# A decoder layer on one core: the second attention pass with two heads' keys on the partitions

## What is computed

```python
x = layernorm(x + block(x))        # rmsnorm, mamba (scan over 1024 steps, 16 states, 1024 inner channels), rmsnorm, SwiGLU
x = layernorm(x + cross(x, ctx))   # attention to 64 context tokens, below
x = layernorm(x + x @ W.T + b + lora)   # dense layer and a top-2 mixture of 8 rank-16 adapters

# cross attention, 16 heads of 32 channels, 64 keys
qk = einsum('bhqd,bhkd->bhqk', Q, K)
scores = qk / sqrt(32)
feats = [scores.mean((q, k)), scores.max(k).mean(q), var(softmax(scores), k).mean(q)]   # per batch and head
t = exp(clip(mlp(feats), -log 10, log 10))
attn = softmax(qk / (2 * t))
out = einsum('bhqk,bhkd->bhqd', attn, V) -> linear Wo, bo
```

## Time and profile before

| | |
|---|---|
| median of 3 runs | 4376.36 us (4375.86 to 4382.17) |
| profiled execution | 4379.0 us, span 4377.2 us |
| PE busy | 3725.6 us, 85% of the span, 9848 matmul records |
| VectorE busy | 2522.7 us, 58% |
| ScalarE busy | 2161.6 us, 49% |
| GpSimd busy | 2488.3 us, 57% |
| granted TensorE clock, mean | 0.901 of full speed |

### The profile page before, as it was taken

How to read it: one execution, slowest core, us unless ns; L and a number is a source line. 1 busy time by engine, 2 the same in 40 slices (tenths; PEclk the granted TensorE clock), 3 DMA queues, 4 the chain that set the end, 5 groups by cost and what they waited for, 6 DMA issues and landing times.

```text
span 4377.2 us, 36093 instructions
## 1 busy us (share of the span) xinstructions
PE 3725.6 (85%) x9848; PEld 1749.1 (40%) x9848; DVE 2522.7 (58%) x3319; ACT 2161.6 (49%) x5177; POOL 2488.3 (57%) x1100
## 2 busy tenths in 40 slices
PE   6555999799979988899999998899998988899677
PEld 3111434343334334544344334534444333544344
DVE  2665478657756883367735885267744886122211
ACT  3443454565465454556526555466526554443344
POOL 0998399649954993079914994059932996000000
PEclk9555999899989998899999998899999998899788
DMA  4333344334523541144423442134423442112000
GB/s 147 115 113 101 104 155 156 111 120 154 164 95 113 164 157 59 63 140 144 152 86 111 155 153 77 63 121 147 146 84 103 160 154 89 40 57 67 25 21 28
DMA packets 221267, 483.17 MB, mean 110 GB/s; under 512 B 31884, under 2 KB 32268, under 8 KB 220812
## 3 DMA queue, kind: packets, MB, share of 16 engines
q1 hardware_dynamic: 221068, 480.87, 34.3%
HBM read 470.82 MB, written 9.96 MB: 110 GB/s over the span
## 4 chain that ended last, share of the span: by engine, by line
PE 54%; POOL 16%; DVE 12%; issue 8%; ACT 8%; DMA 1%; SPq 0%; POOLq 0%; DVEq 0%; ACTq 0%
PE ps L1490 28%; POOL hb L961 10%; DVE hb L1296 6%; POOL hb L951 6%; PE ps L1579 5%; PE ps L1548 5%; PE ps L1591 5%; PE ps L1658 1%; PE ps L1624 1%; PE ps L1603 1%; PE ps L1541 1%; PE ps L1518 1%; ACT ps L1171 1%; PE ps L1670 1%; PE ps L1559 1%
## 5 line engine op out<-in xcount | busy, mean ns | idle before, releaser
L951 POOL TENSOR_TENSOR hb<-dtu,bc 128x1024 f32<-128x1024 f32 x512 | 1205.6, 2356 | 73.3 <-PE ps L1591 31.0
L961 POOL TENSOR_TENSOR hb<-hb,bc 128x1024 f32<-128x1024 f32 x512 | 1205.6, 2355 | 60.7 <-ACT state L1086 35.4
L1490 PE MATMUL ps<-fT,wden 128*128 128x512 f32 x2304 | 1053.6, 607 | 28.6 <-DVE hm L1334 21.1
L1010 ACT ACTIVATE ps<-dt,a_neg 128x512 f32<-128x512 f32 x1024 | 690.9, 688 | 693.3 <-DVE hb L1296 690.2
L1591 PE MATMUL ps<-hb,ident 128*128 128x512 f32 x1024 | 632.4, 706 | 306.3 <-POOL hb L961 303.4
L1490 PEld LDWEIGHTS ps<-fT,wden 128*128 128x128 f32 x2304 | 444.2, 195 | 597.2 <-issue 596.4
L1296 DVE TENSOR_TENSOR_SCAN hb<-ps,state,hb 128x512 f32<-128x512 f32 x512 | 626.7, 1266 | 14.1 <-ACT ps L1010 7.2
L1296 DVE TENSOR_TENSOR_SCAN hb<-ps,hb 128x512 f32<-128x512 f32 x512 | 596.2, 1206 | 21.1 <-POOL hb L951 13.4
L1305 DVE TENSOR_TENSOR ps<-ps,hb 128x512 f32<-128x512 f32 x512 | 355.5, 694 | 364.8 <-POOL hb L961 363.9
L1579 PE MATMUL ps<-wden,hm 128*128 128x512 f32 x1024 | 487.7, 623 | 17.5 <-DVE res L1350 12.8
L1490 PE MATMUL ps<-xnT,wmix 128*128 128x512 f32 x1024 | 468.6, 609 | 12.8 <-ACT xnT L1034 8.7
(11 more groups left out here) (192 smaller groups left out, 3894.4 us busy)
## 6 DMA issues: line engine op xcount, KB each, us to landing
bc<-bc_dram SPq DMA_DIRECT2D x1024, 256.0 KB, 3.7
wden<-in_w SPq DMA_DIRECT2D x192, 512.0 KB, 3.7
wmix<-in_w_mix SPq DMA_DIRECT2D x96, 512.0 KB, 3.6
watt<-in_w_qof SPq DMA_DIRECT2D x32, 512.0 KB, 4.3
xm<-in_x SPq DMA_DIRECT2D x8, 1024.0 KB, 5.5
res<-in_x SPq DMA_DIRECT2D x8, 1024.0 KB, 5.6
wden<-in_w_qof SPq DMA_DIRECT2D x16, 512.0 KB, 3.8
out<-res SPq DMA_DIRECT2D x8, 1024.0 KB, 4.3
```

What stands on the lines that cost most here:

```text
L951: TTn(hb[:, k % 4], dtu[:, :, :], bc[:, 0, k % 3].unsqueeze(1).broadcast_to([P, 2, CH]), ALU.mult).then_inc(s.s1_ready, 1)
L961: TTn(hb[:, k % 4], hb[:, k % 4], bc[:, 1, k % 3].unsqueeze(1).broadcast_to([P, 2, CH]), ALU.mult).then_inc(s.s3_done, 1)
L1010: A_(dst, dt[:, p % 2, jj], ACT.Exp, scale=a_neg[:, j, n:n + 1]).then_inc(full_of(key), 1)
L1490: ins = M(dst, a, b, start=start and n == 0, stop=stop and n == len(pairs) - 1)
```

## The change

The second pass works on 256 queries and two heads at a time, with the 128 keys of the two heads on the partitions.

- `sc2` (now four units for each 256 queries) makes the scores of two pairs of heads. Each pair takes one matmul with `kbd` as the stationary operand and one of 16 rows, which adds minus the maximum of each query and head: `w_dt` rows 64 to 79 and 96 to 111 hold the identity, each of its columns repeated 64 times, and `mxT` the negated maxima with the heads on the partitions.
- `shift`, new, makes `mxT`: four transposes of `mxs` and one copy on ScalarE for each chunk.
- `e2` does two exponentials of 256 columns in place in PSUM, with the scale of the two heads as a column, waits for itself, and copies 512 columns to `at` (Relu). The additions into `den`, `flip` and `nm2` are gone.
- `val` does each of its eight matmuls twice with the same stationary operand: one against `two` (two columns of ones and zeros, which gives the sums over the keys of each head) and one against `vbd`. The sums take a PSUM bank of their own, and `on` reads them with one more VectorE instruction.
- `vbd` has one buffer instead of two; its load is a unit of its own in the DMA list (`v_load`), which waits for the last `val` of the batch element before.
- The planner's costs and dependencies of these units are new, and so the order changes in many places.

```diff
-        got.append(("ent", c))
+        got += [("ent", c), ("shift", c)]
...
-        def e2(t, hf):
-            return [("e2", c, t, hf, 0), ("e2", c, t, hf, 1)]
-        got += [("sc2", c, 0, 0), *e2(0, 0), ("sc2", c, 0, 1), *e2(0, 1)]
-        for t in range(TT):
-            more = t + 1 < TT
-            got += [("flip", c, t, 0), ("flip", c, t, 1)] + ([("sc2", c, t + 1, 0)] if more else [])
-            got += [("val", c, t), ("on", c, t)] + ([("sc2", c, t + 1, 1), *e2(t + 1, 0)] if more else [])
-            got += [("fl2", c, t)] + (e2(t + 1, 1) if more else []) + [("wo", c, t), ("woa", c, t)]
+        for q in range(TT // 2):
+            got += [("sc2", c, q, 0), ("sc2", c, q, 1), ("e2", c, q, 0), ("sc2", c, q, 2), ("e2", c, q, 1), ("sc2", c, q, 3),
+                    ("e2", c, q, 2), ("e2", c, q, 3)]
+            for t in (2 * q, 2 * q + 1):
+                got += [("val", c, t), ("on", c, t)] + ([("wo", c, t - 1), ("woa", c, t - 1)] if t % 2 else []) + [("fl2", c, t)]
+            got += [("wo", c, 2 * q + 1), ("woa", c, 2 * q + 1)]
...
+    elif kind == "shift":
+        part(PE, 0.5, ("ent", c), ("sc2", c - 2, 1, 3), takes=(u,))
+        part(ACT_, EV, mine(), gives=(u,))
     elif kind == "sc2":
-        part(PE, TURN, ("temper", 2 * b + 1), takes=(u,))
+        part(PE, 2 * MM, ("temper", 2 * b + 1), ("shift", c), ("val", c, 2 * i - 1) if i else ("val", c - 1, last), takes=(u,))
     elif kind == "e2":
-        part(ACT_, 2.5, ("sc2", *u[1:4]), ("flip", c, i - 1, u[3]) if i else ("lora", c - 1), ("val", c, i - 2),
-             gives=(("sc2", *u[1:4]),) if u[4] else ())
-    elif kind == "flip":
-        part(PE, 0.65, ("e2", *key, 1), takes=(u,))
-        part(ACT_, EV, mine(), ("val", c, i - 1), gives=(u,))
+        part(ACT_, 1.6, ("sc2", *key), ("fin", c - 1, last), gives=(("sc2", *key),))
     elif kind == "val":
-        part(PE, 1.7, ("flip", c, i, 0), ("flip", c, i, 1), takes=(u,))
+        part(PE, 2.2, ("e2", c, i // 2, 3), takes=(u, ("den", c, i)))
...
+        got.append((DONE[("val", 2 * b - 1, TT - 1)], 2, ("v_load", b)))
...
+            def load_v(b):
+                sp.wait_ge(s.zeroed, 2)
+                if b:
+                    filled(sp, ("val", 2 * b - 1, TT - 1))
                 vv = v_dram[b].rearrange("k (a e d) -> k a e d", e=2, d=DK)
                 for e in range(2):
-                    sp.dma_start(vbd[64 * e:64 * e + 64, r, :, DK * e:DK * e + DK], vv[:, :, e, :]
-                                 ).then_inc(kv_in[r], 16)
+                    sp.dma_start(vbd[64 * e:64 * e + 64, :, DK * e:DK * e + DK], vv[:, :, e, :]).then_inc(v_in, 16)
...
+                elif kind == "shift":
+                    if c > 1:
+                        filled(act, ("sc2", c - 2, 1, 3))
+                    rows = slice(64 + 32 * half, 64 + 32 * half + HEADS)
+                    A_(mxT[rows, :], filled(act, unit)[0:HEADS], ACT.Copy, scale=-1.0).then_inc(free_of(unit), 1)
                 elif kind == "e2":
-                    hf, q = unit[3], unit[4]
-                    key = ("sc2", c, i, hf)
-                    bank = filled(act, key).rearrange("p (h k) -> p h k", k=KEYS)
-                    if q == 0:
+                    n = unit[3]
+                    bank = filled(act, ("sc2", c, i, n))
+                    if n == 0 and i == 0:
                         act.wait_ge(s.tempered, b + 1)
-                    if q == 0 and hf == 0:
-                        if i >= 2:
-                            emptied(act, ("val", c, i - 2))
-                        elif c:
-                            emptied(act, ("val", c - 1, TT - 2 + i))
-                    for h in range(4 * q, 4 * q + 4):
-                        hh = 8 * hf + h
-                        ins = A_(eb[:, hh], bank[:, h], ACT.Exp, bias=nm2[:, TT * half + i, hh:hh + 1],
-                                 scale=ftv[:, 0, hh:hh + 1], accum_out=den[:, 0, i % 2, hh:hh + 1])
-                    if q:
-                        ins.then_inc(free_of(key), 1)
-                elif kind == "flip":
-                    hf = unit[3]
-                    if hf == 0 and i:
-                        filled(act, ("val", c, i - 1))
-                    key = ("flip", c, i, hf)
-                    A_(at[:, hf * 512:(hf + 1) * 512], filled(act, key), ACT.Relu).then_inc(free_of(key), 1)
+                    for m in range(2):
+                        ins = A_(bank[:, m * 256:(m + 1) * 256], bank[:, m * 256:(m + 1) * 256], ACT.Exp,
+                                 scale=ftc[:, 2 * n + m:2 * n + m + 1])
+                    ch.link(ins)
+                    A_(at[:, 2 * n:2 * n + 2], bank.rearrange("p (m q) -> p m q", m=2), ACT.Relu
+                       ).then_inc(free_of(("sc2", c, i, n)), 1)
...
+                    total = ("den", c, i)
+                    V.tensor_scalar(den[:, 0], filled(dve, total)[:, 0:HEADS], 0.5, None, ALU.max).then_inc(free_of(total), 1)
+                    emptied(dve, total)
+                    ch.link(V.reciprocal(den[:, 1], den[:, 0]))
...
+                elif kind == "shift":
+                    dst = take(pe, unit)
+                    pe.wait_ge(s.mx_ready, 2 * TT * (c + 1))
+                    for t in range(TT):
+                        ins = turn(dst[0:HEADS, t * P:(t + 1) * P], mxs[:, TT * half + t], ident[:, :])
+                    ins.then_inc(full_of(unit), 1)
...
+                elif kind == "sc2":
+                    emptied(pe, ("shift", c))
+                    rows = slice(64 + 32 * half, 64 + 32 * half + HEADS)
+                    dst = take(pe, unit)
+                    for m in range(2):
+                        pair = 2 * unit[3] + m
+                        M(dst[:, m * 256:(m + 1) * 256], kbd[:, b % 2, pair // 2, pair % 2 * P:pair % 2 * P + P],
+                          qT[:, pair // 2, half * CH + i * 256:half * CH + i * 256 + 256], start=True, stop=False)
+                        ins = M(dst[:, m * 256:(m + 1) * 256], w_dt[rows, pair * P:(pair + 1) * P], mxT[rows, i * 256:(i + 1) * 256],
+                                start=False, stop=True)
+                    ins.then_inc(full_of(unit), 1)
...
-                elif kind == "flip":
-                    hf = unit[3]
-                    emptied(pe, ("sc2", c, i, hf))
-                    src = eb.rearrange("p h k -> p (h k)")
+                elif kind == "val":
+                    for n in range(4):
+                        emptied(pe, ("sc2", c, i // 2, n))
+                    pe.wait_ge(v_in, 32 * (b + 1))
                     dst = take(pe, unit)
-                    for m in range(4):
-                        ins = turn(dst[:, m * P:(m + 1) * P], src[:, (4 * hf + m) * P:(4 * hf + m + 1) * P], ident[:, :])
-                    ins.then_inc(full_of(unit), 1)
-                elif kind == "val":
-                    for hf in range(2):
-                        emptied(pe, ("flip", c, i, hf))
-                    dst = take(pe, unit)
+                    total = take(pe, ("den", c, i))
                     for m in range(8):
-                        ins = M(dst[:, m * 64:(m + 1) * 64], at[:, m * P:(m + 1) * P], vbd[:, b % 2, m], start=True, stop=True)
+                        probs = at[:, m, i % 2 * P:(i % 2 + 1) * P]
+                        both = M(total[:, 2 * m:2 * m + 2], probs, two[:, :], start=True, stop=True)
+                        ins = M(dst[:, m * 64:(m + 1) * 64], probs, vbd[:, m], start=True, stop=True)
+                    both.then_inc(full_of(("den", c, i)), 1)
                     ins.then_inc(full_of(unit), 1)
...
+    for k in (64, 96):
+        w_dt[k:k + HEADS] = np.repeat(np.eye(HEADS, dtype=f32), KEYS, axis=1)
```

More of the change, by code:

```diff
@@ L428, in ready @@
         if p[5]:
[L429 removed]
+            if len(free) < len(p[5]):
                 return None
[L431 removed]
+            t = max(t, sorted(free.values())[len(p[5]) - 1] + HOP)
         return t
@@ L856, in load_kv @@
                 if b > 1:
-                    for hf in range(2):
-                        filled(sp, ("sc2", 2 * b - 3, TT - 1, hf))
-                    filled(sp, ("val", 2 * b - 3, TT - 1))
+                    for n in range(4):
+                        filled(sp, ("sc2", 2 * b - 3, 1, n))
                     sp.wait_ge(s.kb_sum, b - 1)
@@ L922, in _ @@
                     load_kv(c)
+                elif kind == "v_load":
+                    load_v(c)
                 elif kind == "store":
@@ L939, in _ @@
             nc.gpsimd.memset(t_w2[:, HID:P], 0.0).then_inc(s.zeroed, 1)
+            for e in range(2):
+                pool.wait_ge(s.zeroed, 8 + 2 * e)
+                nc.gpsimd.memset(two[64 * e:64 * e + 64, e:e + 1], 1.0).then_inc(s.zeroed, 1)
+                pool.wait_ge(s.zeroed, 9 + 2 * e)
+                nc.gpsimd.memset(two[64 * e:64 * e + 64, 1 - e:2 - e], 0.0).then_inc(s.zeroed, 1)
             TTn = nc.gpsimd.tensor_tensor
@@ L1374, in _ @@
                     hf = unit[3]
```

(20 more changed lines are left out.)

45 lines of the change are left out of this document (22 added, 23 removed).

## The result

The changed kernel takes 4543.5 us (median of four runs, 4537.57 to 4555.07) beside 4376.1 for the kernel before on the same chip: ratio 1.0383, 95% interval 1.036 to 1.0405. It is 167 us slower. The forecast was 4381 us, in a range from 4361 to 4404, so it was wrong.

A forecast was written before the change was run, and what follows sets the result against it. GpSimd was taken to bound the scans, PE's chain the stretches between, and PE the part behind the mixer. Terms 4.5 + 2.6 + 5 + 0.5 - 7 - 1 = +4.6 us gave 4381 us, range 4361 to 4404.

The forecast's parts named there:

- I price the 16-row matmul as one of 128 rows, since no row shows one so thin: In `sc2` on PE: four matmuls at the 128-row price, 1.72 us a unit instead of 0.86.
- 86 us of PE work fall mostly in scans with idle PE: Over the whole kernel: PE's added work, 10.7 us a chunk, mostly fits where PE idles during scans.
- the clock: Second pass of chunk 6: half clock until 4171.4, then full; bounds for chunks 6 and 7 together 0 to 16 us.
- in the scans: Scans: idle PE takes the added work and less ScalarE work wins nothing; -1 us, from -6 to +25.
- behind scans 3 and 5: After these scans: second passes of chunks 0 and 2 stand in PE's chain; +2 us each.
- behind scans 4 and 6: After these scans: one `w3` and `lora` move ahead of `out`, shortening the chain; -3.5 us each, -7 together.
- beside the SwiGLU: During chunk 7's SwiGLU, where PE is full: added PE work counts; +5 us, from 3 to 8.
- chunk 6 alone: Second pass of chunk 6 running alone: scores at half clock lead the chain; ends at 4219.0 against 4214.5, +4.5 us.
- chunk 7 alone: Second pass of chunk 7 running alone: `sc2` hidden behind layernorm, first `val` starting at half clock; +2.6 us.
- PE becomes the bound of the scans: Slower rival: GpSimd waits for PE in scans, deciding from 5 us each; 4406 us; chance 0.38 including a milder case.
- The matmuls with ones cost little: Faster rival in `val`: stationary load hidden or shared, each `val` 1.35 us shorter; 4353 us, chance 0.06.
- No difference: Rival for the whole kernel: terms cancel to within 0.2%; 4372 to 4385 us, chance 0.44.

The follow-up runs named there:

- run 2: Changed kernel with the 16-row shift matmul of `sc2` taken over 128 rows, 4488.5 us, or over 64 rows, 4536.4 us.
- run 4: Changed kernel with the ones as a column beside the values, so `val` is eight matmuls of 66 columns: 4448.7 us.
- the best version: Changed kernel with `val` as eight matmuls of 66 columns and the shift matmul in bfloat16 over 128 rows, zero-filled: 4362.1 us.

## Why the prediction was wrong

**The step that failed first: "I price the 16-row matmul as one of 128 rows, since no row shows one so thin".** The bound on the other side was nothing; a price *above* a 128-row matmul was not thought of, nor one laid on its neighbours. And a row was there. Timeline of PE in the kernel before, a matmul of 64 rows (`dt`'s projection) between two of 128, all of 512 columns:

```profile
2915.47 1.02 PE L1591 MATMUL ps<-hb,ident 128*128 128x512 f32 x2
2916.33 3.60 PE L1490 MATMUL ps<-fT,wden 128*128 128x512 f32 x8
2919.86 1.12 PE L1541 MATMUL ps<-proj,w_dt 64*128 64x512 f32 x2
2920.91 1.13 PE L1591 MATMUL ps<-hb,ident 128*128 128x512 f32 x2
2921.87 3.60 PE L1490 MATMUL ps<-fT,wden 128*128 128x512 f32 x8
```

128 rows: 0.86 us to the next (2915.47 to 2916.33). 64 rows: 1.05, and the 128-row one behind it 0.96 (2920.91 to 2921.87). By these, two of each in a unit would have been 1.72 + 2 x 0.19 + 2 x 0.10 = 2.3; with 0.2 us for each of the four changes it is 2.5, as measured. What it cost: run 2 puts it at 55 us.

**The step that failed by more: "86 us of PE work fall mostly in scans with idle PE".** The numbers of the run contradict it at its base. Of the 32 `val`, 8 stand in scans of the changed kernel, 8 behind the scans of 3 and 5, and 16 behind scan 7; of the 64 `sc2`, 20 stand in scans. The prediction had numbers against it too: its 7 to 9 us more in each of five scans are some 40 of the 86, and one of its rivals counts 21 of the 32 `val` on the path. For the `val` the price at the full clock was right (3.46; measured 3.5), and still the ones cost 95 us: 1.8 us at the full clock, 3.4 at the half (6.8 against 3.4 for a `val` without them). 54% of their records ran at the half: an estimate from these is 32 x 2.7 = 86 us of PE, about what run 4 gave back in time.

**The step that was mis-sized: the clock.** The forecast let it rise in the pass of chunk 6 as before, at 4171.4, and priced all `val` behind at the full clock; a lower clock stood in the bounds with at most 16 us for both passes. It rose 39.4 us behind the first `sc2`, fell again for 30.7 us in the second half, and each of the four `val` took 6.7 to 6.85 us.

In medians the loss adds up from the runs (they come from several chips, on which the kernel before measured 4374.5 to 4378.1, so each term is good to 2 or 3 us at best): 16 rows instead of 128, 55.0 us (4543.5 to 4488.5); the shift matmul at 128 rows, 25.1 (to 4463.4); the ones, 95.2 (to 4368.2); the rest of the change, -7.9. Sum 167.4.

**Term by term,** in the profiled runs. ScalarE's part was right, and so was `v_load`, hidden: GpSimd waited 22.5 us for `bc` loads, 26.0 before.

| term | forecast | measured | from |
|---|---|---|---|
| in the scans | -1 | +46.8 | the table of scans |
| behind scans 3 and 5 | +4 | +30.5 | the same |
| behind scans 4 and 6 | -7 | -3.3 | the same; `out` to `turn_out` of chunk 6 is 3.4 us shorter, 4 forecast |
| behind scan 7 | -3.7 | +21.6 | scan's end to `turn_out`, 173.3 for 151.7 |
| beside the SwiGLU | +5 | +9.4 | `turn_out` to the first `sc2` of chunk 6's pass, 329.1 for 319.7 |
| chunk 6 alone | +4.5 | +36.5 | 91.9 for 55.4; scores 32.4 and not some 20, four `val` 27.2 and not 13.8 |
| chunk 7 alone | +2.6 | +23.5 | last `wo` of chunk 6 to its own, 129.7 for 106.2 |
| the end | none | +1.9 | what is left of the tail's 92.9 |

Two small slips of the sum change nothing: the three odd scans add up to +0.3, not +0.5, and the 19.1 us in chunk 6's chain are 18.7 by its own list.

**The rivals.** "PE becomes the bound of the scans" had the right sign and a right mechanism, with its mark of 5 us a scan passed in chunks 3, 4 and 6; but it is 47 us of 167, and it put the scans first where the tail is. What GpSimd waits for, after, then in the best version (line waited for: us, times, longest):

```profile
POOL hb L971 <- ACT state L1096: 59.2, 34, 3.8
POOL hb L961 <- PE ps L1596: 50.5, 39, 5.8
```
```profile
POOL hb L970 <- ACT state L1095: 42.3, 33, 3.1
POOL hb L960 <- PE ps L1598: 26.1, 30, 2.0
```

Before, they were 35.4 and 31.0. "The matmuls with ones cost little" is refuted by the records 0.11 us apart. "No difference" rested on chains of 54.2 against 53 us, made from prices at the full clock alone.

What stays open: in these 14 kernels the first rise came later wherever matmuls of few rows stood among the scores, and the clock also fell within the `val` of passes without them. Which feature of the work decides, these runs don't tell. Nor do they split the ones' 95 us between their own time and what they did to the clock of their neighbours.

## What to carry to other kernels

Price a matmul by its neighbours too: here each change of the row count between matmuls cost 0.2 us at the full clock and 0.3 at the half. So fill up to 128 rows with zeros, which paid best here, or keep the thin ones together. Sums by ones belong as extra columns into the matmul that has the same stationary operand. And before work is called hidden, count in the order how many of its units stand where the engine is idle; here a quarter to a third did.

## What the runs showed of the hardware

- A float32 matmul of 256 columns takes 0.43 us among others with 128 rows, 0.63 beside one with 16 or 64 rows, whichever operand is the stationary one; 0.86 and 1.15 at the half clock.
- Two columns with a stationary operand loaded anew cost as much as 66: 0.11 us a record on the mean at the full clock, 0.21 at the half.
- From the start of a pass with 16- or 64-row matmuls among its scores the granted clock stayed at 0.50 for 25 to 39 us, while PE was busy 87 to 92% of the time; without them it first rose after 4.5 to 12 us. In `val` with two-column matmuls, all over 128 rows, it stood at 0.50 for 20.4 us with PE busy 93%.
- A bfloat16 matmul of 128 rows and 256 columns, accumulated in the same bank between float32 ones, takes 0.11 us in this run of matmuls; with 16 rows it took 0.21, and its neighbours 0.1 more.
